# A GpSimd indirect step waits for the landing of the step two ahead of it

## Chip, cores and metric

One core of one Trainium2 chip runs the whole program. The metric is the device time in microseconds, median of the runs. TensorE is called PE in the rows, VectorE DVE, ScalarE ACT, GpSimd POOL and SyncE SP.

## The reference, cut to what matters

Two transformer layers run over x of 32 batches x 256 tokens x 128 features. Layer 0 is an RWKV mixer and an FFN. Layer 1 is a 16-head attention and a mixture of 8 experts, of which each token takes 2. Each of the four parts has its own modulation (shift, scale and gate by batch). The change lies in the experts' part, which the reference states densely:

```
for e in range(NUM_EXPERTS):
    expert_mask = jnp.any(top_idx == e, axis=-1)
    h = jax.nn.relu(flat_x @ W1[e] + b1[e])
    y = h @ W2[e] + b2[e]
    w = router_weights[:, e] * expert_mask.astype(x.dtype)
    final_output = final_output + y * w[:, None]
```

## The kernel before

The 8192 tokens are 16 chunks of 512 (NT = 4 tiles of 128). Every engine walks an order written out by hand (ORDER, a list of named steps for each engine), and waits only on semaphores. A step's number below is its place among the steps of its name. Steps of the letters A, E, B, C, G and R are layer 0, the attention and the router; they fill the span up to about 1435 us, and the experts' steps are mixed in from about 560 us on.

The experts' part works in four groups of 5, 5, 4 and 2 chunks, which have 47, 47, 39 and 23 tiles of 128 slots.

- S_slot (DVE, L1693) computes the slot of every token's two copies, once a group is routed.
- S_ld (SP, L603) loads the normed chunk into sx, two buffers. S_sc (POOL, L751) scatters it to x_slots in DRAM: two steps a chunk, one for each choice of expert, and each step is four indirect DMAs, one for each tile of 128 rows of 512 bytes.
- M_ldx (SP, L615) loads four slot tiles (a quad), after every scatter of its group has landed. M_w (SP, L628) loads one tile's expert weights. M_t (PE, L1048) turns a quad, M_u (PE, L1023) and M_d (PE, L1036 and L1040) are the tile's two products, and M_st (SP, L632) stores the quad to y_slots. Tiles 133 to 155 and quads 34 to 39 are the last group's.
- K_g (POOL, L770) gathers a chunk's rows from y_slots into kg: again two steps of four indirect DMAs a chunk, after every M_st of the chunk's group has landed. K_sum and K_out (DVE, L1717 to L1731) weigh, add and gate them, K_st (SP, L647) stores the output. K_ldx (SP, L642 and L643) loads the residual chunk and its gate.
- The gathers have four buffers (kg, the halves of bhs, and bqk), but chunks 0 to 9 all use the first. Chunks 10, 11 and 12 take the other three, 13 the first again, then 14 and 15 those of 10 and 11. The first step of a chunk waits until its buffer's last output is stored (k_st).

POOL has one walk over all 64 indirect steps: S_sc0-19, K_g0-9, S_sc20-27, K_g10-13, S_sc28, K_g14, S_sc29, K_g15, S_sc30, S_sc31, K_g16-31. The steps K_g28 to K_g31 belong to the last group and have no such wait; every other step, before its first DMA, waits in landed() for the step just ahead of it in this walk:

```
walk = [k for k in steps("Pool") if k[0] in ("S_sc", "K_g")]
return dict(zip(walk[1:], walk))
```

In SP's order the steps of this stage stand in one queue. From the middle of the tail: M_ldx33 M_w126 M_w127 K_st7 K_ldx8 M_w128 M_w129 M_ldx34 M_st30 M_w130-136 M_st31 K_st8 M_w137 M_ldx35 M_w138 M_st32 M_w139 K_ldx9 K_ldx10 M_ldx36 M_st33 M_w140-143 M_ldx37 K_ldx11 M_st34 M_w144 K_ldx12 K_ldx13 M_w145 M_st35 M_ldx38 M_w146-152 K_st9 M_ldx39 M_w153 K_ldx14 M_w154 K_st10 K_ldx15 K_st11 M_st36 M_w155 M_st37 K_st12 M_st38 M_st39 K_st13 K_st14 K_st15.

Of the kernel before, what the change touches and what calls it, by code (L numbers as in the profile page):

```python
# [13 lines left out]
ACT = mybir.ActivationFunctionType  # L14
# [7 lines left out]
NT = N // P  # L22
# [11 lines left out]
SIZES = (5, 5, 4, 2)  # L34
# [11 lines left out]
FIRST_CHUNK = [sum(SIZES[:g]) for g in range(GROUPS)]  # L46
# [37 lines left out]
e_dx e_xr e_xk e_xv e_r e_th e_k e_v e_ky e_m e_exp e_dv e_att e_wo e_x1 e_norm e_tp e_xn  # L84
e_fk e_rl e_sq e_fr e_th2 e_vk e_aq e_y e_ga e_out
b_ldm b_norm b_tp b_h b_w1 b_hs b_w2 b_x2 b_st b_q b_k b_t b_qk b_p b_r b_stq b_v b_va
c_ldq0 c_ldq1 c_rows0 c_rows1 c_s c_mx c_mp c_mt c_mT c_s2 c_p c_pv c_o c_ot c_ctx c_ct c_cT c_wo c_y c_ldm c_st
r_ldm r_z0 r_h0 r_hn r_tp r_h r_rt r_lg r_dm r_e r_info r_sth
s_zero s_tot s_pre s_base s_slot s_tile s_ldx0 s_ldx1 s_sc0 s_sc1
m_ldx0 m_ldx1 m_ldx2 m_ldx3 m_ldx4 m_ldx5 m_st0 m_st1 m_st2 m_st3 m_st4 m_st5 m_w0 m_w1 m_w2 m_w3 m_w4 m_w5 m_w6 m_w7 m_w8 m_w9 m_w10 m_w11 m_w12 m_w13 m_tp m_x m_h m_r m_y m_o  # L90
k_ld0 k_ld1 k_ld2 k_ld3 k_g0 k_g1 k_g2 k_g3 k_sum k_out k_st0 k_st1 k_st2 k_st3
vec
""".split()

# [49 lines left out]
def indirect_before():  # L144

    walk = [k for k in steps("Pool") if k[0] in ("S_sc", "K_g")]
    return dict(zip(walk[1:], walk))

class Count:  # L150
# [13 lines left out]
def program(nc, a):  # L164
    ctx = ExitStack()
    with ctx:
# [211 lines left out]
        def k_set(c):  # L378

            return k_sets[c], k_sets[:c + 1].count(k_sets[c])  # L380
# [33 lines left out]

        def scattered(g, k):

            return 16 * 2 * NT * len([c for c in range(FIRST_CHUNK[g] + SIZES[g]) if c % 2 == k])

        def rows(dram, i):
            return dram[i * N:(i + 1) * N, :].rearrange("(t p) d -> p t d", p=P)  # L420
# [4 lines left out]
        with nc.Block() as block:  # L425
# [63 lines left out]
            def _(sp):  # L489
                for s, i in steps("SP"):  # L490
# [108 lines left out]
                    if s == "S_ld":  # L599
                        sp.wait_ge(S["r_sth"], 16 * (i + 1))  # L600
                        if i >= 2:
                            sp.wait_ge(S[f"s_sc{i % 2}"], 16 * 2 * NT * (i // 2))
                        sp.dma_start(sx[:, i % 2, :, :], rows(x_h, i)).then_inc(S[f"s_ldx{i % 2}"], 16)  # L603

                    if s == "M_ldx":
                        g, t, j, n = first_of(i)
                        for k in range(2):
                            sp.wait_ge(S[f"s_sc{k}"], scattered(g, k))
                        k, use = x_slot(i)
                        if use > 1:  # L610
                            sp.wait_ge(S[f"m_st{k}"], 16 * (use - 1))
                        elif k >= MXS:

                            sp.wait_ge(S["e_vk"], 2 * CHUNKS)
                        sp.dma_start(quads[k][:, 0:n, :], x_slots[g][j * P:(j + n) * P, :]  # L615
                                     .rearrange("(t p) d -> p t d", p=P)).then_inc(S[f"m_ldx{k}"], 16)
# [36 lines left out]
            def _(pool):  # L653
# [10 lines left out]
                def landed(s, i):  # L664

                    if (s, i) not in before_:
                        return
                    s_, i_ = before_[s, i]
                    c_, k_ = divmod(i_, 2)
                    if s_ == "S_sc":  # L670
                        pool.wait_ge(S[f"s_sc{c_ % 2}"], 16 * NT * (2 * (c_ // 2) + k_ + 1))
                    if s_ == "K_g":
                        z_, n_ = k_set(c_)
                        pool.wait_ge(S[f"k_g{z_}"], 16 * NT * (2 * (n_ - 1) + k_ + 1))

                for s, i in steps("Pool"):
                    if s == "I_set":
# [64 lines left out]
                    if s == "S_sc":  # L742
                        c, k = divmod(i, 2)
                        if i == 0:
                            pool.wait_ge(S["s_zero"], 16 * GROUPS)
                        if k == 0:
                            pool.wait_ge(S["s_slot"], GROUP_OF[c] + 1)
                            pool.wait_ge(S[f"s_ldx{c % 2}"], 16 * (c // 2 + 1))
                        landed(s, i)
                        for t in range(NT):  # L750
                            pool.indirect_dma_start(  # L751
                                out=x_slots[GROUP_OF[c]],
                                out_offset=bass.IndirectOffsetOnAxis(ap=sslot[:, c, k, t:t + 1], axis=0),
                                in_=sx[:, c % 2, t, :], in_offset=None).then_inc(S[f"s_sc{c % 2}"], 16)
                    if s == "K_g":
                        c, k = divmod(i, 2)
                        z, n = k_set(c)
                        if k == 0:
                            for m in range(len(quads)):
                                if stored(GROUP_OF[c], m):  # L760
                                    pool.wait_ge(S[f"m_st{m}"], stored(GROUP_OF[c], m))
                            if n > 1:
                                pool.wait_ge(S[f"k_st{z}"], 16 * (n - 1))
                            elif z:

                                pool.wait_ge(S["r_h0"], CHUNKS)
                        if GROUP_OF[c] < GROUPS - 1:
                            landed(s, i)
                        for t in range(NT):
                            pool.indirect_dma_start(  # L770
                                out=kg[z][:, k, t, :], out_offset=None, in_=y_slots[GROUP_OF[c]],
                                in_offset=bass.IndirectOffsetOnAxis(ap=sslot[:, c, k, t:t + 1], axis=0)
                            ).then_inc(S[f"k_g{z}"], 16)

            @block.scalar
            def _(act):
# [7 lines left out]
                for s, i in steps("Activation"):  # L784
# [120 lines left out]
                    if s == "G_ct":  # L905
                        act.wait_ge(S["c_ct"], i + 1)
                        if i:
                            act.wait_ge(S["c_wo"], i)
                        act.activation(ccT[:, :], CO[:, :], ACT.Copy).then_inc(S["c_cT"], 1)

                    if s == "R_h":
                        act.wait_ge(S["r_tp"], i + 1)
# [34 lines left out]
            def _(pe):  # L947
# [109 lines left out]
                for s, i in steps("PE"):  # L1057
# [166 lines left out]
                                            cP[:, (4 * i + g) % 8, :], start=(sc_ == 0), stop=(sc_ == 1))  # L1224
                        ins.then_inc(S["c_pv"], 1)
                    if s == "G_o":
                        pe.wait_ge(S["c_o"], i + 1)
                        for j in range(4):
                            ins = pe.transpose(CO[:, j * P:(j + 1) * P], cos_[:, j * P:(j + 1) * P], ident[:, :])
                        ins.then_inc(S["c_ot"], 1)  # L1230
# [5 lines left out]
                                               ident[:, :])  # L1236
                        ins.then_inc(S["c_ct"], 1)
                    if s == "G_wo":
                        pe.wait_ge(S["c_cT"], i + 1)
                        bias_rows(CO, BO)  # L1240
                        for t in range(NT):
                            ins = pe.matmul(CO[:, t * P:(t + 1) * P], ccT[:, t * P:(t + 1) * P], woT[:, :],
# [38 lines left out]
            def _(dve):  # L1281
# [42 lines left out]
                for s, i in steps("DVE"):  # L1324
# [387 lines left out]
                    if s == "K_sum":  # L1712
                        k, n = k_set(i)
                        g_, w_ = kg[k], rinfo[:, i, :, :]
                        dve.wait_ge(S[f"k_g{k}"], 16 * 2 * NT * n)
                        for t in range(NT):
                            v(dve.tensor_scalar(g_[:, 0, t, :], g_[:, 0, t, :], w_[:, t, P1:P1 + 1], None, ALU.mult))  # L1717
                        v.wait()
                        for t in range(NT):
                            ins = dve.scalar_tensor_tensor(g_[:, 0, t, :], g_[:, 1, t, :], w_[:, t, P2:P2 + 1],  # L1720
                                                           g_[:, 0, t, :], ALU.mult, ALU.add)
                        ins.then_inc(S["k_sum"], 1)
                    if s == "K_out":
                        k, n = k_set(i)
                        g_ = kg[k]
                        dve.wait_ge(S["k_sum"], i + 1)
                        dve.wait_ge(S[f"k_ld{k}"], 32 * n)
                        v(dve.tensor_tensor(by_batch(g_[:, 1, :, :]), by_batch(g_[:, 0, :, :]),
                                            per_batch(km[k], g_), ALU.mult))
# [290 lines left out]
```

## Time and profile before

| | us |
|---|---|
| median of 3 runs | 1640.79 (1640.04 to 1642.62) |
| the profiled execution | 1635.33, its span 1633.4 |
| PE busy | 1352.7 (83%) |
| DVE busy | 1093.5 (67%) |
| ACT busy | 993.4 (61%) |
| POOL busy | 544.0 (33%) |

Times of rows are microseconds from the span's start. The shares of busy time are means over stages with different limits; the last 200 us are a stage of their own, without DVE's and ACT's layer work.

### The profile page before, as it was taken

Reading aid. Unit: us, or ns where it says so; the run is one execution under the profiler, and the core shown is the slowest. Engines: PE = TensorE matmul, PEld = TensorE weight load, DVE = VectorE, ACT = ScalarE, POOL = GpSimd, SP = SyncE. Lnnn points to the kernel's source line nnn. Section 1 sums busy time; section 2 is a strip of 40 time slices with the busy share of each in tenths; the row PEclk is TensorE's granted clock in tenths of the full one; section 3 lists DMA queues with packets and bytes.
Section 4 is the critical chain, followed back from the end, with each engine's and each line's share of the span. In section 5 each row is a group of like instructions: output and inputs, shape, how many; then the busy total and the mean of one; then the engine's idle time right before and its main releaser. Section 6 shows DMA issues by size and latency. Waiting matters only on the chain.

```text
span 1633.4 us, 26721 instructions
## 1 busy us (share of the span) xinstructions
PE 1352.7 (83%) x8354; PEld 857.3 (52%) x8354; DVE 1093.5 (67%) x2943; ACT 993.4 (61%) x2295; POOL 544.0 (33%) x589
## 2 busy tenths in 40 slices
PE   3366997888888778999999988999989998986680
PEld 1233443544444444767666543466656655776570
DVE  4568889898788988767677888778846644220113
ACT  1354766577575647787787675677666666653350
POOL 1133213222122465121212137725430144334345
PEclk7677888978899889999999998899999999998795
DMA  4012134215240333446455432345656566886872
GB/s 125 7 36 68 48 106 141 81 31 158 57 127 23 108 100 103 132 146 179 137 155 151 126 106 78 117 118 177 171 157 188 171 189 206 273 268 216 242 230 75
DMA packets 202036, 217.67 MB, mean 133 GB/s; under 512 B 17418, under 2 KB 167525, under 8 KB 199592
## 3 DMA queue, kind: packets, MB, share of 16 engines
q1 hardware_dynamic: 193704, 199.18, 40.7%
q0 software_dynamic: 8192, 16.79, 3.3%
q8 instruction: 68, 1.11, 0.3%
q14 instruction: 72, 0.59, 0.1%
HBM read 161.18 MB, written 53.94 MB: 132 GB/s over the span
## 4 chain that ended last, share of the span: by engine, by line
PE 37%; DVE 13%; issue 9%; POOL 8%; DMA 6%; ACT 5%; another core or an unknown queue 0%; SPq 0%; POOLq 0%; ACTq 0%; DVEq 0%
PE bank L1040 6%; PE bank L1223 5%; PE bank L1207 4%; PE bank L1023 4%; PE bank L1191 3%; DVE cmx L1576 3%; POOL kg L770 3%; DMA kg<-y_slots,sslot 3%; POOL x_slots L751 2%; DMA x_slots<-sx,sslot 2%; PE bank L1159 2%; POOL bhs L770 2%; PE bank L1119 1%; PE bank L1146 1%; PE bank L1167 1%
## 5 line engine op out<-in xcount | busy, mean ns | idle before, releaser
L1576 DVE TENSOR_REDUCE cmx<-bank 128x2 f32<-128x512 f32 x512 | 328.2, 682 | 89.5 <-PE bank L1191 82.8
L898 ACT ACTIVATE wide<-bank 128x512 f32<-128x512 f32 x512 | 281.2, 607 | 74.0 <-PE bank L1207 63.9
L1207 PE MATMUL bank<-wide 75*128 75x512 bf16 x512 | 179.5, 416 | 25.5 <-DVE cmx L1576 14.6
L1191 PE MATMUL bank<-wide 72*128 72x256 bf16 x1024 | 180.7, 284 | 23.8 <-DVE cmx L1576 20.4
L751 POOL DMA_INDIRECT x_slots<-sx,sslot x128 | 127.2, 994 | 111.8 <-issue 36.2
L1191 PEld LDWEIGHTS bank<-wide 72*128 72x128 bf16 x1024 | 91.5, 101 | 135.3 <-issue 62.5
L1223 PE MATMUL bank<-wide,bva 128*32 128x512 f32 x1024 | 144.2, 642 | 3.3 <-ACT wide L898 1.9
L937 ACT ACTIVATE mH<-bank,mW 128x128 f32<-128x128 f32 x376 | 107.8, 376 | 60.5 <-PE bank L1023 55.6
L1023 PE MATMUL bank<-mT,mW 128*128 128x128 f32 x872 | 120.2, 281 | 12.7 <-DMA mW<-in_wexp 6.7
L1023 PEld LDWEIGHTS bank<-mT,mW 128*128 128x128 f32 x872 | 108.7, 193 | 33.1 <-issue 11.9
L1207 PEld LDWEIGHTS bank<-wide 75*128 75x128 bf16 x512 | 49.5, 105 | 133.2 <-ACT wide L898 62.0
L770 POOL DMA_INDIRECT kg<-y_slots,sslot x88 | 85.7, 974 | 99.1 <-issue 34.0
L658 POOL TENSOR_TENSOR brs<-bvar,half 128x4 f32<-128x4 f32 x32 | 33.8, 1057 | 243.3 <-DVE bvar L1292 243.2
L1040 PE MATMUL bank<-mW,mH 128*128 128x128 f32 x752 | 108.9, 288 | 0.0
L1146 PE MATMUL bank<-bh,w 128*128 128x512 f32 x128 | 85.8, 758 | 13.8 <-ACT bhs L874 7.5
L1040 PEld LDWEIGHTS bank<-mW,mH 128*128 128x128 f32 x752 | 91.0, 191 | 6.3
L944 ACT ACTIVATE mX<-bank 128x128 f32<-128x128 f32 x120 | 33.6, 280 | 91.3 <-PE bank L1040 82.2
L730 POOL TENSOR_TENSOR bqk<-bqk,bp 128x768 f32<-128x768 f32 x32 | 53.5, 1672 | 103.7 <-ACT bp L884 103.6
L1119 PE MATMUL bank<-axk,fwk 128*128 128x512 f32 x128 | 70.7, 661 | 11.9 <-DVE axk L1295 10.2
L1717 DVE TENSOR_SCALAR kg<-kg,rinfo 128x128 f32<-128x128 f32 x44 | 9.7, 284 | 102.8 <-DMA kg<-y_slots,sslot 102.8
L874 ACT ACTIVATE bhs<-bank,col 128x512 f32<-128x512 f32 x64 | 44.3, 693 | 43.2 <-PE bank L1146 42.9
L1159 PE MATMUL bank<-w,bhs 128*128 128x128 f32 x512 | 65.6, 284 | 0.0
(296 smaller groups left out, 2801.1 us busy)
## 6 DMA issues: line engine op xcount, KB each, us to landing
mW<-in_wexp SPq DMA_DIRECT2D x109, 514.0 KB
wide<-q_parts SPq DMA_DIRECT2D x32, 576.0 KB
inner<-in_wexp SPq DMA_DIRECT2D x31, 514.0 KB
wide<-in_wexp SPq DMA_DIRECT2D x16, 514.0 KB, 5.5
mX<-x_slots SPq DMA_DIRECT2D x27, 256.0 KB
y_slots<-mX SPq DMA_DIRECT2D x27, 256.0 KB
q_parts<-bp SPq DMA_DIRECT2D x32, 192.0 KB
x_slots<-mH SPq DMA_DIRECT2D x2, 3072.0 KB, 11.0
```

The source lines that it names most:

```text
L751: pool.indirect_dma_start(out=x_slots[GROUP_OF[c]], out_offset=bass.IndirectOffsetOnAxis(ap=sslot[:, c, k, t:t + 1], axis=0), in_=sx[:, c ...
L770: pool.indirect_dma_start(out=kg[z][:, k, t, :], out_offset=None, in_=y_slots[GROUP_OF[c]], in_offset=bass.IndirectOffsetOnAxis(ap=sslot[: ...
L898: act.activation(cP[:, i % 8, :], bank[seat["G_s", i]][:, :], ACT.Exp, scale=SCALE).then_inc(S["c_p"], 1)
L937: act.activation(hidden[z][:, c * P:(c + 1) * P], bank[seat[k]][:, c * P:(c + 1) * P], ACT.Relu, bias=w_[:, FC * P + c:FC * P + c + 1]).th ...
L1023: ins = pe.matmul(ps[:, c * P:(c + 1) * P], weights[w_][:, c * P:(c + 1) * P], mT[:, q % 2, j * P:(j + 1) * P], start=True, stop=True)
L1040: ins = pe.matmul(ps[:, 0:P], hidden[z][:, c * P:(c + 1) * P], weights[w_slot(i)[0]][:, o:o + D], start=False, stop=(c == FC - 1))
L1146: pe.matmul(ps[:, :], w1[:, j * P:(j + 1) * P], bh[:, :], start=True, stop=True).then_inc(S["b_w1"], 1)
L1159: ins = pe.matmul(ps[:, t * P:(t + 1) * P], bhs[:, c, t * P:(t + 1) * P], w2[:, c, :], start=False, stop=(c == FC - 1 and t == NT - 1))
L1191: ins = pe.matmul(ps[:, j * T:(j + 1) * T], cQ[0:SROWS, z, h, tt * P:(tt + 1) * P], cK[0:SROWS, z, h // G, :], start=True, stop=True)
L1207: pe.matmul(ps[:, :], cK[0:KROWS, z, g, sc_ * P:(sc_ + 1) * P], cQ[0:KROWS, z, h0:h0 + 2, :], start=True, stop=True).then_inc(S["c_s2"], 1)
L1223: ins = pe.matmul(CO[32 * g:32 * g + 32, :], bva[:, c % 2, b * 2 + sc_, g, :], cP[:, (4 * i + g) % 8, :], start=(sc_ == 0), stop=(sc_ == 1))
L1576: dve.tensor_reduce(cmx[:, u % 2, tt, 2 * hp:2 * hp + 2], bank[seat["C_s", i]][:, :].rearrange("p (j t) -> p j t", j=2), AX_X, ALU.max, ne ...
```

## The change

Three edits go together. indirect_before() pairs each indirect step with the step two ahead in the walk, so two steps may be in flight. Because steps of one chunk may then land in either order, each half (k = 0 or 1) of a chunk parity has a semaphore of its own: s_sc00 to s_sc11 for the scatters, k_g00 to k_g11 for the gathers, which were counted by buffer. As a k_g semaphore is now shared by buffers, the first step of a chunk c from the third chunk on waits for K_out of chunk c - 2. To pay for the semaphores, k_sum and c_cT go: K_out waits on DVE's own counter, and the copy of G_ct counts on c_o.

```
-    return dict(zip(walk[1:], walk))
+    return dict(zip(walk[2:], walk))
...
-                            sp.wait_ge(S[f"s_sc{i % 2}"], 16 * 2 * NT * (i // 2))
+                            for k in range(2):
+                                sp.wait_ge(S[f"s_sc{i % 2}{k}"], 16 * NT * (i // 2))
...
-                            sp.wait_ge(S[f"s_sc{k}"], scattered(g, k))
+                            for j_ in range(2):
+                                sp.wait_ge(S[f"s_sc{k}{j_}"], scattered(g, k))
...
-                        pool.wait_ge(S[f"s_sc{c_ % 2}"], 16 * NT * (2 * (c_ // 2) + k_ + 1))
+                        pool.wait_ge(S[f"s_sc{c_ % 2}{k_}"], 16 * NT * (c_ // 2 + 1))
...
-                        z_, n_ = k_set(c_)
-                        pool.wait_ge(S[f"k_g{z_}"], 16 * NT * (2 * (n_ - 1) + k_ + 1))
+                        pool.wait_ge(S[f"k_g{c_ % 2}{k_}"], 16 * NT * (c_ // 2 + 1))
...
+                            if c >= 2:
+
+                                pool.wait_ge(S["k_out"], c - 1)
...
-                        act.activation(ccT[:, :], CO[:, :], ACT.Copy).then_inc(S["c_cT"], 1)
+                        act.activation(ccT[:, :], CO[:, :], ACT.Copy).then_inc(S["c_o"], 1)
...
-                        pe.wait_ge(S["c_o"], i + 1)
+
+                        pe.wait_ge(S["c_o"], i + i // 4 + 1)
...
-                        pe.wait_ge(S["c_cT"], i + 1)
+                        pe.wait_ge(S["c_o"], 5 * (i + 1))
...
-                        dve.wait_ge(S[f"k_g{k}"], 16 * 2 * NT * n)
+                        for j_ in range(2):
+                            dve.wait_ge(S[f"k_g{i % 2}{j_}"], 16 * NT * (i // 2 + 1))
...
-                        ins.then_inc(S["k_sum"], 1)
+                        v(ins)
...
-                        dve.wait_ge(S["k_sum"], i + 1)
+                        v.wait()
```

## Rows read from the trace of the kernel before

**Rows 1.** The page's chain that ended last, share of the span by engine.

```profile
PE 37%; DVE 13%; issue 9%; POOL 8%; DMA 6%; ACT 5%; another core or an unknown queue 0%; SPq 0%; POOLq 0%; ACTq 0%; DVEq 0%
```

**Rows 2.** Windows: stretch, its us, busy us by engine (instructions), clock, DMA share, GB/s.

```profile
1405.00:1477.00 72.00, 63.88 (x486) 56.26 (x486) 19.36 (x77) 41.17 (x144) 26.09 (x27) 1.00 0.87 270
...
1477.00:1592.00 115.00, 84.22 (x573) 72.95 (x571) 17.30 (x52) 46.95 (x169) 45.99 (x48) 0.88 0.72 228
1592.00:1633.00 41.00, 0.00 (x0) 0.00 (x0) 13.54 (x39) 0.00 (x0) 23.30 (x24) 0.51 0.26 75
```

**Rows 3.** Waits of POOL, 1405 to 1634: us in total, times, longest.

```profile
POOL kg L770 <- DMA kg<-y_slots,sslot: 15.6, 4, 5.8
POOL bhs L770 <- DMA bhs<-y_slots,sslot: 14.0, 3, 5.2
...
POOL kg L770 <- DMA x_slots<-sx,sslot: 9.3, 3, 4.1
...
POOL x_slots L751 <- DMA kg<-y_slots,sslot: 7.8, 2, 4.1
...
POOL x_slots L751 <- DMA x_slots<-sx,sslot: 3.9, 1, 3.9
```

**Rows 4.** Timeline of POOL: S_sc28, K_g14, K_g16, K_g18 and K_g28 begin.

```profile
1445.81 1.01 POOL L751 DMA_INDIRECT x_slots<-sx,sslot  x1 [11.69 <-DVE sslot L1693]
...
1454.70 0.97 POOL L770 DMA_INDIRECT kg<-y_slots,sslot  x1 [4.05 <-DMA x_slots<-sx,sslot]
...
1497.33 0.97 POOL L770 DMA_INDIRECT kg<-y_slots,sslot  x1 [2.06 <-DMA x_slots<-sx,sslot]
...
1520.34 0.94 POOL L770 DMA_INDIRECT kg<-y_slots,sslot  x1 [8.21 <-DMA out_dram<-kg]
...
1605.36 0.94 POOL L770 DMA_INDIRECT bhs<-y_slots,sslot  x1 [0.30 <-issue]
```

**Rows 5.** Chain: last DMA of K_g17, K_g19 and K_g31, start and us to landing.

```profile
1511.19 2.43 DMA kg<-y_slots,sslot
...
1534.51 6.30 DMA kg<-y_slots,sslot
...
1624.61 2.43 DMA bhs<-y_slots,sslot
```

**Rows 6.** Timeline of SP: M_w126/127, K_st7, M_ldx34, K_st8, M_ldx35, K_st9, K_st12.

```profile
1471.71 3.24 SPq L628 DMA_DIRECT2D inner<-in_wexp  x2
1482.69 0.40 SPq L647 DMA_DIRECT2D out_dram<-kg  x1
...
1496.60 0.38 SPq L615 DMA_DIRECT2D mX<-x_slots  x1
...
1517.17 0.40 SPq L647 DMA_DIRECT2D out_dram<-kg  x1
...
1518.80 0.36 SPq L615 DMA_DIRECT2D mX<-x_slots  x1
...
1562.03 0.43 SPq L647 DMA_DIRECT2D out_dram<-kg  x1
...
1595.21 0.38 SPq L647 DMA_DIRECT2D out_dram<-bqk  x1
```

**Rows 7.** Timeline of PE: M_u128, M_t35, M_u155 and the last matmuls.

```profile
1490.17 1.56 PE L1023 MATMUL bank<-mT,mW 128*128 128x128 f32 x8 [4.10 <-DMA mW<-in_wexp]
...
1522.92 1.09 PE L1048 MATMUL bank<-ident,mX 128*128 128x128 f32 x4 [10.38 <-DMA mX<-x_slots]
...
1587.81 1.13 PE L1023 MATMUL bank<-mT,mW 128*128 128x128 f32 x8 [2.61 <-DMA mW<-in_wexp]
...
1590.33 1.16 PE L1040 MATMUL bank<-mW,axr 128*128 128x128 f32 x8
```

**Rows 8.** First group's scatters: POOL's wait, 555 to 640; PE's timeline.

```profile
POOL x_slots L751 <- DMA x_slots<-sx,sslot: 12.8, 5, 5.3
```

```profile
613.37 3.70 PE L1119 MATMUL bank<-axk,fwk 128*128 128x512 f32 x4 [4.98 <-DVE axk L1295]
```

More of the change, by code:

```diff
@@ L86 @@
 b_ldm b_norm b_tp b_h b_w1 b_hs b_w2 b_x2 b_st b_q b_k b_t b_qk b_p b_r b_stq b_v b_va
-c_ldq0 c_ldq1 c_rows0 c_rows1 c_s c_mx c_mp c_mt c_mT c_s2 c_p c_pv c_o c_ot c_ctx c_ct c_cT c_wo c_y c_ldm c_st
+c_ldq0 c_ldq1 c_rows0 c_rows1 c_s c_mx c_mp c_mt c_mT c_s2 c_p c_pv c_o c_ot c_ctx c_ct c_wo c_y c_ldm c_st
 r_ldm r_z0 r_h0 r_hn r_tp r_h r_rt r_lg r_dm r_e r_info r_sth
-s_zero s_tot s_pre s_base s_slot s_tile s_ldx0 s_ldx1 s_sc0 s_sc1
+s_zero s_tot s_pre s_base s_slot s_tile s_ldx0 s_ldx1 s_sc00 s_sc01 s_sc10 s_sc11
 m_ldx0 m_ldx1 m_ldx2 m_ldx3 m_ldx4 m_ldx5 m_st0 m_st1 m_st2 m_st3 m_st4 m_st5 m_w0 m_w1 m_w2 m_w3 m_w4 m_w5 m_w6 m_w7 m_w8 m_w9 m_w10 m_w11 m_w12 m_w13 m_tp m_x m_h m_r m_y m_o
-k_ld0 k_ld1 k_ld2 k_ld3 k_g0 k_g1 k_g2 k_g3 k_sum k_out k_st0 k_st1 k_st2 k_st3
+k_ld0 k_ld1 k_ld2 k_ld3 k_g00 k_g01 k_g10 k_g11 k_out k_st0 k_st1 k_st2 k_st3
 vec
@@ L415, in scattered @@
         def scattered(g, k):
-            return 16 * 2 * NT * len([c for c in range(FIRST_CHUNK[g] + SIZES[g]) if c % 2 == k])
+            return 16 * NT * len([c for c in range(FIRST_CHUNK[g] + SIZES[g]) if c % 2 == k])
         def rows(dram, i):
@@ L753, in _ @@
                                 out_offset=bass.IndirectOffsetOnAxis(ap=sslot[:, c, k, t:t + 1], axis=0),
-                                in_=sx[:, c % 2, t, :], in_offset=None).then_inc(S[f"s_sc{c % 2}"], 16)
+                                in_=sx[:, c % 2, t, :], in_offset=None).then_inc(S[f"s_sc{c % 2}{k}"], 16)
                     if s == "K_g":
@@ L772, in _ @@
                                 in_offset=bass.IndirectOffsetOnAxis(ap=sslot[:, c, k, t:t + 1], axis=0)
-                            ).then_inc(S[f"k_g{z}"], 16)
+                            ).then_inc(S[f"k_g{c % 2}{k}"], 16)
             @block.scalar
```

## Prediction

> **What bounds the kernel now.** I read the chain that ended last first. PE carries 37% of it, POOL and the DMAs 14% together [rows 1], and asked by stretch these 14% lie in two places: the first group's scatters (555 to 610 us) and everything after 1420 us. The windows show the second: up to 1477 PE is busy 64 of 72 us, from 1477 to 1592 only 84 of 115 us, and in the last 41 us not at all, while the DMA engines, at 0.87 of their time before 1477, fall to 0.72 [rows 2]. So the tail waits for something that is neither PE nor bandwidth. POOL's own waits name it: landings of its indirect DMAs, 50.6 us in these five groups of 13 waits [rows 3]. The reader is to see in POOL's timeline that a step is 4.84 us of issuing (1445.81 to 1454.70 less the 4.05 of waiting), and that the next one starts only after a landing [rows 4]. The chain shows what a landing is, from the start of a step's last DMA: 2.43 us twice, 6.30 us in the busiest stretch [rows 5].
>
> PE is tied to this chain through SP's queue, in which loads for PE stand behind stores for POOL. K_st7 held SP from 1474.95 (the end of the weight issues ahead of it) to 1482.69; M_ldx34 waited for the last scatter until 1496.60; K_st8 held it until 1517.17, with M_ldx35 1.6 us behind [rows 6]. PE pays 4.10 us for the first, 10.38 us for the last, and 2.61 us at the end [rows 7].
>
> **The change part by part.** Four issues stay four issues; nothing is added to POOL but waits. Each step in place of "step ahead has landed" waits "step two ahead has landed", which leaves a whole step of issuing (5.0 to 5.1 us with the 0.3 us gap) for the landing. The step after the next can begin 1.25 + 5.0 = 6.25 us after the start of a step's last DMA, so a landing of 2.43 us is hidden entirely and one of 6.30 us costs next to nothing, if two steps in flight land as one does. Bounds for the landing: 2.43 below, 6.30 above [rows 5].
>
> The first gain is at the scatters. S_sc28 starts at 1445.8 as before, since DVE's slots release it [rows 4]. Six steps (S_sc28, K_g14, S_sc29, K_g15, S_sc30, S_sc31) at 5.1 us are issued by 1476.4, and the last scatter has landed by 1478 to 1482, where it was 1496.6 [rows 6]. M_ldx34 goes out some 15 us earlier, before PE, which would come to it at about 1491, needs it.
>
> The second is at K_st7. Chunk 7's gathers are issued by 1466.2 (four steps) and land 2.4 to 6.3 us after the last one's start. From K_g17's landing (1511.19 + 2.43) to K_st8 (1517.17) lie 3.55 us of DVE and SP [rows 5, 6], so K_out7 is done by 1472 to 1475 and SP issues K_st7 at once, at 1475. From K_st8 to K_g18 took 3.2 us [rows 4, 6], so K_g16 starts at 1478.2 instead of 1497.3. M_w128 leaves 7.7 us earlier, and PE's 4.10 us go.
>
> The third, and the one that counts, is at K_st8. K_g16 and K_g17 run without a wait between them: the last DMA starts 9.0 us later, at 1487.2, lands at 1489.7 to 1493.5, and K_st8 goes at 1493.2 to 1497.1, which is 20 to 24 us earlier. M_ldx35 follows 1.6 us later and M_t35 4.1 us after that [rows 6, 7], 1499 to 1503. PE itself, without its 4.10 us, comes to M_t35 at 1486.1 plus five tiles at 2.7 us (62 us for 23 tiles, worked out in the next paragraph), 1499.6. So the 10.38 us become 0 to 3, and the last group's tiles start at 1500 to 1504, not at 1523.8.
>
> Its 23 tiles took from 1523.8 to 1591.5, 67.7 us. Off this go the 2.61 us of M_w155, which K_ldx15 and K_st11 held back, and part of the slow clock that followed the 10.38 us of idling: the granted clock was 0.88 in this stretch against 1.00 before [rows 2, 7]. I take 3 us for it, with 0 as its low end. That is 62 us, or 65 without the clock's part, so that PE ends between 1562 and 1569. The DMA engines speak against the low end. They worked 0.72 x 115 = 83 us between 1477 and 1592; the same bytes at the 0.87 of the stretch before take 95 us, until 1572 [rows 2]. I take 1570.
>
> From there: the last quad's store goes about 1 us after PE's end (K_st12, which held it until 1595.2, is ready long before), and K_g28 starts 3.2 us after it, at 1574 where it was 1605.4. From K_g28's start to the span's end are 16 issues, a landing, DVE and a store: 1633.4 - 1605.4 = 28.0 us [rows 4], with no landed wait in them, so unchanged. The end is 1602, 31 us earlier.
>
> POOL's own chain must be ready by then. K_g18 starts at 1497 to 1500, eight steps at 5.0 us take it to 1540, K_g26 then waits for K_st9, which SP reached 38.2 us after M_u133 [rows 6], now 1541, plus 3.2; K_g27 is issued by 1554. That is 20 us of slack: POOL would have to need 7.5 us a step before it sets the end.
>
> Upstream the waits are shorter and mostly covered. In the first group POOL waits 12.8 us for landings, and PE then stands 4.98 us for the chain that goes through the POOL step behind them [rows 8]. S_sc6 also needs S_ld3, which SP issues at about the old time, so I take 2.5 us of the 4.98. The three other groups' waits lie beside a busy PE; I count 0 to 2 us, below 0 nothing, as no wait is longer there. With half a microsecond: 2 to 3 us.
>
> The rest costs nothing that I can price. S_ld and M_ldx wait on two semaphores for one, in the 1.2 us that SP needs anyway between K_st8 and M_ldx35 [rows 6]; below 0.1 us each. K_out(c - 2) is implied by the buffer's store up to chunk 10, and in chunks 11 to 15 it is 3.5 us behind a gather whose landing is 5 us past: what is queued behind it (K_g) finds it met. K_out's wait is on its own engine. The renamed c_o counts wait for what stands earlier in PE's order.
>
> Of a DMA's length the Trainium skill ("DMA: Bandwidth & Descriptors", section "Anatomy of one DMA") says about 2.0 us fixed, most of it the receipt of the last write, plus bytes over 436e3. For 64 KB that is an estimate of 2.15 us. The unloaded rows of 2.43 agree and the loaded one of 6.30 doesn't [rows 5]; by the page alone K_st8 would go at 1493, inside the bounds above.
>
> The sum: 31 + 2.5 = 33 us off. It is made against the profiled execution's 1635.33 (span 1633.4, 1.9 us around it), which lies 5.5 us below the median of the runs; 1640.8 - 33 = 1608. The likeliest case's own range is 1598 (PE 1562, upstream 4) to 1617 (all high ends, SP losing a few us more).
>
> **The rivals.** A, the software queue is served at a rate and not after a latency: K_g19's four DMAs took 3.75 us of issues and 6.30 more, 10 us, and if under load that is 2.5 us of service each, a second step in flight only queues behind the first. What remains of each removed wait is the gap from a landing to the next issue, about 1 us with its first DMA's latency. The 13 waits give 13 us [rows 3], 1628. For it speaks that the long landings lie where DMA is busiest; against it that K_g28 to K_g31 issue 16 DMAs at 1.25 us and the last lands in 2.43 all the same [rows 5], though at a DMA share of 0.26 [rows 2]. 
>
> B, the weight loads become the bound: the tail's last 28 tiles are short of bandwidth, at the 228 GB/s that the stretch had on average [rows 2], and PE ends at 1580 to 1588. K_g28 at 1588 gives 17 us and upstream 2: 1621.
>
> C, slower: the denser scatters and gathers take so much from the weight loads after 1445 that PE ends later than it did. The price is known: PE would have to lose more than the 31 us over 28 tiles, 1.1 us on each 2.9, that is a rate down from 228 to 165 GB/s, where the stretches before show 270. From there on it decides, not earlier.
>
> D, no change: something else holds SP at K_st7 and K_st8 (the residual loads, or landings over 10 us when two steps share the queue), and the pair of steps lasts what it lasted. 1640.
>
> **How the numbers follow.** The main case 0.68, A 0.13, B 0.13, C 0.03, D 0.03. Faster by over 0.2% (3.3 us, about what these runs tell from no change) are the first three, 0.94; within it 0.03; slower 0.03. The range goes from the main case's low end to A's time with its bounds: 1597 to 1629.
>
> **What would show it.** After 1445 POOL's steps follow each other by 5.0 to 5.5 us, with waits for landings under 12 us in total where they were 50.6. K_st8 stands at about 1495, M_t35 has no wait above 4 us, the DMA share between 1477 and PE's end is over 0.85, and K_g28 is released by the store of the last quad and not by POOL. If landings go to 10 us it is A; if PE waits for mW, inner or wide over the last group it is B. I am wrong if K_st8 is later than 1505.

## The result, and the profile after

The changed kernel took 1695.20 us (median of 4 runs, 1691.56 to 1696.52), the kernel before 1640.76 beside it: a ratio of 1.0338 with a 95% interval of 1.0319 to 1.0358. That is 54 us slower, where 33 faster were forecast. The profiled execution took 1694.17 us (span 1692.4).

The page's chain by engine comes first; [rows 1] had nothing for an unknown queue and 14% for POOL and DMA.

```profile
PE 46%; DVE 12%; ACT 8%; another core or an unknown queue 6%; issue 6%; POOL 1%; DMA 1%; SPq 0%; POOLq 0%; ACTq 0%; DVEq 0%
```

POOL and the DMAs are nearly off the chain, but 6% (some 100 us) is put down to nothing that the profile knows. The waits of the changed kernel (us in total, times, longest) name who it is. "Remote" stands where the profile finds no instruction and no DMA that ended just before the wait did; below such waits are called ended by nothing:

```profile
ACT mX L948 <- remote: 54.1, 7, 16.7
...
ACT bhs L878 <- remote: 13.5, 2, 9.2
...
DVE rlg L1631 <- remote: 10.6, 1, 10.6
```

ACT has 112.8 us of such waits and DVE 15.1; SP's queue has 36.1 more, all for PE's line 1044. The timelines of ACT and of PE, around 1500 us, show one (the columns are those of [rows 4]):

```profile
1493.41 0.28 ACT L948 ACTIVATE mX<-bank 128x128 f32<-128x128 f32 x1 [3.65 <-remote]
1493.58 1.14 ACT L941 ACTIVATE axr<-bank,mW 128x128 f32<-128x128 f32 x4
1506.82 0.28 ACT L948 ACTIVATE mX<-bank 128x128 f32<-128x128 f32 x1 [12.10 <-remote]
1506.99 1.14 ACT L941 ACTIVATE axk<-bank,mW 128x128 f32<-128x128 f32 x4
1514.53 0.60 ACT L930 ACTIVATE mT<-bank 128x512 f32<-128x512 f32 x1 [6.40 <-remote]
```

```profile
1494.93 1.80 PE L1044 MATMUL bank<-mW,axr 128*128 128x128 f32 x8
1496.53 1.06 PE L1052 MATMUL bank<-ident,ah 128*128 128x128 f32 x4
1507.15 2.08 PE L1027 MATMUL bank<-mT,inner 128*128 128x128 f32 x8 [9.56 <-ACT mX L948]
```

ACT's copy into mX waits in the program for one thing, the matmuls of line 1044. They end at 1496.73; the copy starts at 1506.82, and PE's next tile, which waits for that copy, 0.3 us behind it. All that time POOL issues indirect DMAs (24 from 1479.90 to 1511.7, the last 20 every 1.25 to 1.5 us without a gap over 0.3 us). The same picture stands at 1588.75 to 1605.44 (16.69 us), beside 24 issued from 1571.25 to 1602.5, and at 578.71 (9.21 us), beside 12. I call this the hold.

**Whose event is late.** The trace also holds the semaphore updates themselves, and they say more than "remote" does. In the recorded run ACT and DVE have 23 such waits of over 1 us, and each is for a semaphore that PE counts up. The update that ends the wait is recorded, within 0.03 us of the start of the waiting instruction; it is late against the matmuls that send it. The one for the copy above is recorded at 1506.80, 10.1 us after their end at 1496.73. Fifty of PE's updates come over 1.5 us after the last matmul that could have sent them, the latest 16.9 us after. ACT's 1,843 and POOL's 322 all come within 0.01 us of their instruction's end. Ends of matmuls are modelled, but the order alone shows it: PE's transposes (line 1052, from 1496.53) were followed by seventeen more matmuls from 1507.15 to 1511.45, and only at 1514.50 is the transposes' update recorded, with two more of PE within 0.2 us and 2.8 us after POOL's last issue. So what is held is PE's semaphore updates. ACT, DVE and SP stand still because they wait for PE.

Of POOL's waits for landings in [rows 3] none is left, and the last landing of the chain is as long as in [rows 5]:

```profile
1682.31 2.44 DMA bhs<-y_slots,sslot
```

PE's waits of 4.10 and 10.38 us [rows 7] have given way to 9.56, 4.92 and 12.67 us for ACT. The rows that answer to [rows 4] and [rows 6], timelines of POOL and of SP:

```profile
1479.90 1.01 POOL L752 DMA_INDIRECT x_slots<-sx,sslot  x1 [12.86 <-DVE sslot L1698]
...
1535.51 0.97 POOL L774 DMA_INDIRECT kg<-y_slots,sslot  x1 [23.85 <-DMA out_dram<-kg]
...
1559.81 0.94 POOL L774 DMA_INDIRECT kg<-y_slots,sslot  x1 [14.58 <-DMA out_dram<-kg]
...
1663.32 0.94 POOL L774 DMA_INDIRECT bhs<-y_slots,sslot  x1 [18.51 <-DMA y_slots<-mX]
```

```profile
1529.95 0.43 SPq L649 DMA_DIRECT2D out_dram<-kg  x1
...
1535.03 0.38 SPq L617 DMA_DIRECT2D mX<-x_slots  x1
...
1552.12 1.14 SPq L649 DMA_DIRECT2D out_dram<-kg  x1
...
1554.59 0.36 SPq L617 DMA_DIRECT2D mX<-x_slots  x1
```

S_sc28 starts 34.1 us later than in [rows 4], K_g28 58.0 later. So 34 us are lost before the tail, most of them (25.8) between 1325 and S_sc28, where 16 indirect DMAs run without a break, and 24 in the tail. The windows, as in [rows 2]:

```profile
1405.00:1477.00 72.00, 63.02 (x460) 50.74 (x459) 19.31 (x82) 41.77 (x130) 18.13 (x19) 0.95 0.76 238
1477.00:1592.00 115.00, 74.01 (x460) 64.37 (x460) 17.23 (x55) 37.46 (x134) 53.82 (x56) 0.77 0.67 214
1592.00:1664.00 72.00, 49.85 (x332) 43.82 (x330) 10.26 (x30) 28.07 (x100) 16.32 (x18) 0.81 0.53 172
```

PE and the DMAs both fell: PE 74.0 us of 115 where it had 84.2, DMA share 0.67 for 0.72. Neither is the bound: PE waits for ACT, the weight loads wait in SP's queue, and PE's granted clock falls from 0.88 to 0.77 with its idling.

### The profile page after: what moved, and what is told of

The parts are those of the page before. It is cut to its first block, busy times and chain, and to the rows that moved or that the text cites. A ratio compares the mean times of both kernels' runs of the same rounds, so it can differ in the third digit from the quotient of the medians.

```text
span 1692.4 us, 26787 instructions
## 1 busy us (share of the span) xinstructions
PE 1375.4 (81%) x8354; PEld 875.1 (52%) x8354; DVE 1094.2 (65%) x2943; ACT 993.4 (59%) x2295; POOL 544.9 (32%) x589
## 4 chain that ended last, share of the span: by engine, by line
PE 46%; DVE 12%; ACT 8%; another core or an unknown queue 6%; issue 6%; POOL 1%; DMA 1%; SPq 0%; POOLq 0%; ACTq 0%; DVEq 0%
PE bank L1044 9%; PE bank L1027 7%; PE bank L1227 5%; PE bank L1211 5%; DVE cmx L1581 4%; PE bank L1195 3%; PE bank L1163 2%; PE bank L1150 2%; PE bank L1123 2%; ACT wide L902 1%; PE bank L1139 1%; PE bank L1040 1%; PE bank L1012 1%; PE bank L1171 1%
## 5 line engine op out<-in xcount | busy, mean ns | idle before, releaser
L1603 DVE RECIPROCAL crs<-bank 128x16 f32<-128x16 f32 x64 | 16.2, 253 | 80.8 <-PE bank L1234 72.5
```

## The experiments

Theory H, in terms of the waits: the other engines are held while POOL issues more than about 8 indirect DMAs without a pause. Rivals: K, the new counts and waits cost it; B, the denser scatters and gathers take bandwidth from the weight loads; and, after the first results, C, it belongs to the chip.

Eighteen runs were made, on six chips, the kernel before beside each. The chips fall into two kinds by three marks that agree in every run: the time of the kernel before (1630 to 1631, or 1641 to 1650), and the last two columns. "Held" is the sum of ACT's and DVE's remote waits in us; "records" is the number of semaphore updates by DMAs that the trace holds.

```
run (chip)               us       before   ratio [95%]              held   records
e5  changed kernel (15)  1584.80  1630.80  0.9728 [0.9703, 0.9753]    0    16,008
e6  7 unlanded     (15)  1586.02  1630.80  0.9732 [0.9714, 0.9749]    0    15,998
e2  6 unlanded     (15)  1592.04  1631.29  0.9755 [0.9739, 0.9772]    0    16,019
e7  5 unlanded     (15)  1605.42  1630.80  0.9853 [0.9836, 0.9871]    0    16,033
e1  one ahead      (15)  1631.47  1631.29  1.0008 [0.9992, 1.0025]    0    16,034
e8  tail one ahead (15)  1624.02  1630.80  0.9962 [0.9949, 0.9976]    0    16,020
e3  1.1 us pause   (15)  1603.08  1631.29  0.9822 [0.9806, 0.9839]    0    16,006
e16 0.2 us break   (12)  1589.08  1630.25  0.9754 [0.9724, 0.9784]    0    16,004
recorded result    (?)   1695.20  1640.76  1.0338 [1.0319, 1.0358]  127.9  11,942
e9  changed kernel  (3)  1711.65  1645.51  1.0400 [1.0351, 1.0450]  138.6  11,877
e10 three ahead     (3)  1708.31  1645.51  1.0395 [1.0349, 1.0442]  128.1  11,889
e12 6 unlanded     (10)  1682.00  1649.94  1.0192 [1.0124, 1.0260]   99.2  11,937
e18 0.2 us break   (13)  1716.55  1646.86  1.0437 [1.0393, 1.0480]  120.9  11,861
e14 1.1 us pause    (5)  1626.50  1641.00  0.9904 [0.9878, 0.9930]   25.2  12,230
e13 3.3 us pause    (5)  1687.12  1641.00  1.0273 [1.0218, 1.0328]    9.7  12,813
bursts: e4 (15) 1626.85, before 1631.29; e17 (12) 1627.63, before 1630.25;
        e11 (10) 1690.39, before 1649.94; e15 (5) 1647.48, before 1641.00
        held 0, 0, 77.1 and 20.4; records 16,586, 16,776, 12,753 and 12,900
```

The updates give a fourth mark. In every run on chips 12 and 15 PE's latest update comes 0.06 us after its matmul. On the others 8 (e13) to 51 (e10) come over 1.5 us late. The kernel before, on the chip on record, has 12, none over 2.2 us. Each burst kernel was timed once. Chip 15 was met twice and every other numbered chip once, so that "the chip" may also be the occasion.

**Is it the bookkeeping?** e1 keeps all of the change but the distance:

```diff
-    return dict(zip(walk[2:], walk))
+    return dict(zip(walk[1:], walk))
```

> The changed kernel with everything kept (counts of their own for the halves, the wait for K_out, the merged counters) except that a step waits for the step one ahead again. Theory H (the hold): while POOL issues more than about 8 indirect DMAs without a pause, ACT, DVE and SP stand still; the loss is in the runs of back-to-back steps alone, so this kernel is at the kernel before, 1640 +- 5 us, and ACT's waits that no engine of the trace ends fall from 95 us and more to about 10. Rival K (the counts): the new waits or merged counters cost it; then this kernel stays near 1695.

1.0008: the separate counts, the wait for K_out and the merged counters cost nothing, as forecast.

**Fewer unlanded, or a pause.** e2 makes a step wait for the step one ahead before its third DMA; e6 does it before the fourth, e7 before the second. e3 puts POOL's own small power ahead of each step that waits.

```diff
                         for t in range(NT):
+                            if t == 2:
+                                landed(s, i, one_ahead)
                             pool.indirect_dma_start(
```

```diff
+                            pool.tensor_tensor(idle_[:, :], onesf[:, 0:NT], half[:, :], ALU.pow)
```

> The changed kernel, in which a step also waits for the step one ahead before its own third DMA, so that at most 6 indirect DMAs are unlanded instead of 8. Theory H in its form 'what counts is how many are unlanded': the waits for nothing in the trace fall to about 10 us, and the time to 1625 to 1645. Theory H in its form 'what counts is that POOL issues without a pause': where a landing takes 2.4 us the third DMA waits for almost nothing, the pauses are 0 to 3 us, and part of the hold stays: 1640 to 1680. Rival B (bandwidth: the denser scatters and gathers take it from the weight loads): it follows the mean rate of issue, which hardly falls, 1680 to 1695.

> The changed kernel with one tiny VectorE-like operation of POOL itself (a power of 128x4, 1.04 us by the rows of such operations) ahead of every step that waits for the one two ahead. It waits for no landing, and two steps are still in flight. Form 'without a pause': a pause of 1.1 us after each 4 DMAs lets the others go on, 1620 to 1650, and ACT's waits for nothing in the trace fall under 20 us. Form 'how many unlanded': 1680 to 1700, since the DMAs in flight are the same. Rival B: 1680 to 1695.

Both were much faster than the kernel before, and no wait in any trace of this chip is remote. Either both mended the hold, or there was none on this chip.

**The hold by itself.** e4 adds gathers that nobody reads to the kernel before.

```diff
+                    for j in range(12):
+                        if apart_ and j and j % 4 == 0:
+                            pool.wait_ge(S["k_g0"], 16 * (12 * n + j))
+                        pool.indirect_dma_start(out=..., in_=x_slots[0], ...)
```

> The kernel before (one step ahead), with 36 gathers added that nobody reads, in three stretches of 26 to 34 us in which POOL was idle while PE, ACT and DVE worked: 12 back to back of 64 KB each, 12 back to back of 4 KB each, and 12 of 64 KB in three lots of 4, each lot after the landing of the lot ahead. Theory H: ACT or DVE stands still for 5 to 10 us, with no engine that ends the wait, in the first and the second burst from about 8 DMAs in, and not in the third; the time rises by 5 to 20 us. Rival B: the 4 KB burst costs nothing, and the third costs about what the first does. If none of the three shows a wait, the hold needs something else that the tail has.

None of the three held anybody, and the time did not rise. This fell against theory H, so the changed kernel had to be timed again beside its neighbours.

> The changed kernel itself, once more, beside its neighbours. With 8 DMAs unlanded and a tiny operation of POOL between steps the time was 1603; with at most 6 unlanded and nothing between, 1592; and 12 gathers back to back in the middle of the kernel held nobody. Theory H (the hold by an unbroken run of indirect DMAs) in what is left of it: it needs a run of over 12, as only this kernel's tail has, and this run gives 1685 to 1700 again, with the waits for nothing. Rival C (the chip or the occasion: the loss belongs to the chip that timed it and not to the kernel): here it gives 1590 to 1610, like its two neighbours.

> The changed kernel with the wait for the step one ahead before a step's fourth DMA, so that at most 7 are unlanded. Between 6 (1592) and 8. Theory H: by then 3.8 us of issuing cover most landings, runs are nearly unbroken, and the time lies between 1592 and 1695, at 1600 to 1660. Rival C: 1588 to 1600, the same as with 6.

> The same with the wait before a step's second DMA: at most 5 unlanded. 1.25 us of a landing of 2.4 to 6.3 us are covered, a third of what 7 cover: both theories give a third to a half of the 39 us that 6 gained, 1605 to 1622.

1584.8: the same program is 2.7% faster here. Its POOL issues 20 indirect DMAs without a break from 1437 us on, and ACT keeps its pace beside them. With 5, 6, 7 and 8 unlanded the time falls from 1605 to 1592, 1586 and 1585; 7 take nearly all that two ahead give. e8 is one ahead again from S_sc28 on:

```diff
+    at = walk.index(("S_sc", 28))
+    return dict(list(zip(walk[2:at], walk)) + list(zip(walk[at:], walk[at - 1:])))
```

> The changed kernel, two ahead up to the scatter of chunk 13, and from the scatters of the last group (S_sc28) on one ahead. Theory H: the long runs are all after 1445 us except one of 12 in the first group, so nearly all of the 54 us goes, 1625 to 1650, and the first group's share alone is left. Rival C: what the tail gained is given back, the first group's 2 to 8 us stay, 1622 to 1632.

1624: so about 7 of the 46 us come from before the tail, and 39 from the tail.

**Another chip.** e9 is the changed kernel once more, e10 waits three ahead.

> The changed kernel a third time. It took 1695 us where it was first timed (kernel before 1641 beside it) and 1585 where the experiments ran (1631 beside it). Theory C (the occasion: one chip's event path loses and delays what indirect DMAs send, the kernel is the faster one elsewhere): 1580 to 1592 if this is the chip of the experiments, and either this or about 1695 on another. Theory H (the kernel's unbroken runs hold the other engines by themselves): 1685 to 1700; after the last run I give it little.

> The changed kernel with each step waiting for the one three ahead: up to 12 indirect DMAs unlanded. If the hold has a threshold of unlanded or unbroken DMAs that lies higher on this chip, it shows here as waits for nothing and a time over 1600. If landings are all that a step waits for, two ahead has hidden them already (0.3 and 0.8 us of such waits are left in its tail), and this one takes the same 1585 within 3 us.

On chip 3 the loss is back, larger than on record, with the same waits:

```profile
ACT mX L948 <- remote: 57.1, 7, 18.5
...
DVE rlg L1631 <- remote: 10.6, 1, 10.6
```

Three ahead is no different from two. So the chip, or the occasion, decides whether there is a hold, and the kernel whether it is met.

**The burst on such a chip.** e11 adds a fourth burst, of 8.

> The burst kernel again (the kernel before, with gathers added that nobody reads, in stretches where POOL was idle beside a working PE, ACT and DVE), now with four: 8 back to back of 64 KB, 12 back to back of 64 KB, 12 back to back of 4 KB, and 12 of 64 KB in lots of 4, each after the landing of the lot ahead. On the chip of the first eight runs 12 back to back held nobody. If this is a chip of the other kind (kernel before at 1640 or more, the changed one 4% slower): theory P (there an unbroken run of indirect DMAs holds the other engines, whatever the bytes) says that ACT or DVE stands still for 3 to 15 us, ended by nothing recorded, beside the two bursts of 12 and not beside the lots of 4, with 8 near the edge. Rival Q (bytes: what these chips lack is DMA bandwidth) says that the 4 KB burst costs nothing. Rival R (only the tail's weight loads together with the gathers do it) says that no burst costs anything.

The starts of the four bursts in POOL's timeline (lines that follow at 1.25 us are left out), then what ACT and DVE waited for in these stretches:

```profile
652.16 1.03 POOL L690 DMA_INDIRECT kg<-x_slots,sslot  x1 [0.53 <-issue]
...
734.86 1.04 POOL L690 DMA_INDIRECT kg<-x_slots,sslot  x1 [0.52 <-issue]
...
833.37 1.04 POOL L690 DMA_INDIRECT kg<-x_slots,sslot  x1 [0.52 <-issue]
...
932.66 1.04 POOL L690 DMA_INDIRECT kg<-x_slots,sslot  x1 [0.52 <-issue]
```

```profile
663.68 0.28 ACT L969 ACTIVATE mX<-bank 128x128 f32<-128x128 f32 x1 [3.35 <-remote]
...
752.10 1.14 ACT L962 ACTIVATE mH<-bank,mW 128x128 f32<-128x128 f32 x4 [5.65 <-remote]
...
849.11 0.28 ACT L969 ACTIVATE mX<-bank 128x128 f32<-128x128 f32 x1 [6.24 <-remote]
```

```profile
744.29 0.69 DVE L1601 TENSOR_REDUCE cmx<-bank 128x2 f32<-128x512 f32 x1 [5.07 <-remote]
...
752.14 0.69 DVE L1601 TENSOR_REDUCE cmx<-bank 128x2 f32<-128x512 f32 x1 [5.03 <-remote]
...
850.55 0.69 DVE L1601 TENSOR_REDUCE cmx<-bank 128x2 f32<-128x512 f32 x1 [15.97 <-remote]
```

On chip 15, in e4, the last of these DVE instructions stood beside the same 4 KB burst like this:

```profile
818.50 0.69 DVE L1600 TENSOR_REDUCE cmx<-bank 128x2 f32<-128x512 f32 x1 [6.27 <-PE bank L1215]
```

Twelve gathers of 4 KB hold DVE for 15.97 - 6.27 = 9.7 us more. The longest remote waits beside the twelve of 64 KB are 5.65 us (ACT) and 5.07 (DVE): rival Q, the bytes, falls. The unbroken 8 hold ACT for 3.35 us. Beside the three lots of 4, each after a landing, DVE has one wait of 3.84 us ended by nothing and ACT none. The whole kernel took 1690 us, 40 more than the kernel before beside it; on chip 15 the three bursts of e4 had cost nothing.

> The changed kernel with the wait for the step one ahead before each step's third DMA, at most 6 unlanded: 1592 on the chip where the changed kernel took 1585. On a chip of the other kind: if the number of unlanded DMAs makes the hold, with 6 instead of 8 most of it goes, 1590 to 1640; if it is POOL's unbroken issuing, the waits of 0 to 3 us in the middle of a step break the run in part, 1620 to 1690; if any rate above that of the kernel before is too much, 1690 to 1710. On the chip of the first runs: 1589 to 1595 again.

1682: two ahead with 6 unlanded is 1.9% slower than the kernel before on chip 10 (1.2 to 2.6%). It pauses only where a landing takes longer than two issues, and its trace has runs of 10 and 12.

**Which pause mends it.** e13 is e3 with three powers in place of one, e14 is e3 again. e15 breaks the bursts in the same way.

> The changed kernel with three tiny operations of POOL's own (1.04 us each, some 3.3 us in all) ahead of each step that waits for the one two ahead: no unbroken run is longer than 4 DMAs. On a chip of the second kind (kernel before at 1640 or more): if a pause in time is what lets the others through, it is at 1600 to 1645 and its trace has under 25 us of waits ended by nothing recorded; if the DMAs have to land first (a landing there takes 2.4 to 6 us), part of the hold stays, 1645 to 1690. On the first chip: a step every 8.3 us, where one ahead took 5.0 and a landing: 1605 to 1625.

> The same with one such operation, 1.1 us: 1603 on the first chip. On a chip of the second kind the step repeats every 6.1 us where the changed kernel's does every 5.0. If the hold grows with the backlog that a rate of over one DMA per some 1.6 to 2 us leaves, a fifth less rate takes a part of it away only: 1650 to 1700. If any break is enough: 1600 to 1645.

> The burst kernel with four bursts of 12 gathers of 64 KB, broken by POOL's own tiny operations (1.1 us each): one after each 4, one after each, three after each 4, two after each 4. On a chip of the second kind, where 12 unbroken ones held ACT and DVE for 5 us twice in one burst and 16 us in another: if a break itself is enough, none of the four holds anybody. If it is the mean rate, the first holds them nearly as long as an unbroken one (15 us of issuing become 17), the fourth for 0 to 5 us, and the second and third (2.4 and 2.1 us per DMA) not at all. On the first chip none holds anybody.

On chip 5 e14 is 1.0% faster than the kernel before, and its waits ended by nothing are 25 us where the unbroken kernels of other chips have 128 to 139. The unbroken kernel itself did not run on chip 5. That the chip is of the second kind is read from its marks, 20 late updates of PE in e14 among them; how long it would hold the unbroken kernel is not shown. In e15 one pause after each 4 leaves ACT and DVE alone beside the burst at 651 us, and beside the third burst (three pauses after each 4) cmx shows its 6.27 us, ended by PE, as on chip 15; beside the fourth, with two pauses, DVE has one such wait, 3.75 us. The expectation of a hold "nearly as long" for the first was wrong. A step of e14 in POOL's timeline:

```profile
1475.03 1.04 POOL L685 TENSOR_TENSOR idle_<-onesf,half 128x4 f32<-128x4 f32 x1
1476.26 1.02 POOL L787 DMA_INDIRECT kg<-y_slots,sslot  x1 [0.19 <-issue]
...
1482.31 1.05 POOL L764 DMA_INDIRECT x_slots<-sx,sslot  x1 [0.19 <-POOL idle_ L685]
```

e13, at 1687, is in the range of "the DMAs have to land first", but not for that reason. Its holds are gone (9.7 us); its steps repeat every 8.3 us whether or not anything has landed, and POOL's own operations stand behind them: ACT's waits for bqk grow from 19.9 us in e14 to 33.3, S_sc28 starts at 1502.6 for 1457.9, and from there to K_g28 it needs 155.7 us for 136.3. Where the rest of the 61 us between the two comes from stays open.

**Rate or break.** e16 and e18 are e14 with a multiplication of 0.2 us in place of the power; e17 breaks the bursts with it.

```diff
-                            pool.tensor_tensor(idle_[:, :], onesf[:, 0:NT], half[:, :], ALU.pow)
+                            pool.tensor_tensor(idle_[:, :], onesf[:, 0:NT], half[:, :], ALU.mult)
```

> The changed kernel with a break of one 0.2 us multiplication of 128x4 on POOL ahead of each step, where 1.1 us gave 1603 on the first chip and 1626 on one of the second kind. By the rows of the bursts a break of 0.2 us leaves the rate at 1.25 us per DMA. If any other instruction between the DMAs is enough to let the others through: no waits ended by nothing recorded, and 1588 to 1598 on the first chip, 1600 to 1620 on one of the second kind. If the rate makes the hold: the first chip as said, and 1670 to 1710 on one of the second kind.

> The burst kernel with four bursts of 12 gathers of 64 KB: broken by a 0.2 us multiplication after each 4, and after each one; by one 1.04 us power after the sixth; and after the eighth. On a chip of the second kind: if the rate makes the hold, the first holds ACT or DVE for 4 to 10 us; if an instruction between is enough, it doesn't, nor does the second; the last holds for 3 to 6 us, as the unbroken 8 did (3.4 us), and the third for 0 to 3. On the first chip none holds anybody.

> The changed kernel with the 0.2 us break once more, which took 1589 (kernel before 1630 beside it) where no hold occurs at all. On a chip of the second kind: 1600 to 1620 and no waits ended by nothing recorded if any instruction between the DMAs lets the others through; 1670 to 1710 if it is the rate of 1.25 us per DMA that holds them. On one of the first kind: 1586 to 1592 again, and the question stays open.

e16 and e17 met a chip of the first kind and could not answer. e18 met one of the second. Its timelines of POOL and ACT:

```profile
1504.14 0.95 POOL L787 DMA_INDIRECT kg<-y_slots,sslot  x1 [0.30 <-issue]
1505.11 0.21 POOL L685 TENSOR_TENSOR idle_<-onesf,half 128x4 f32<-128x4 f32 x1
1505.48 1.01 POOL L764 DMA_INDIRECT x_slots<-sx,sslot  x1 [0.16 <-issue]
```

```profile
1508.92 0.28 ACT L961 ACTIVATE mX<-bank 128x128 f32<-128x128 f32 x1 [4.12 <-remote]
1509.09 1.14 ACT L954 ACTIVATE axr<-bank,mW 128x128 f32<-128x128 f32 x4
1525.97 0.28 ACT L961 ACTIVATE mX<-bank 128x128 f32<-128x128 f32 x1 [15.75 <-remote]
```

On chip 13 a step every 5.1 to 5.5 us (about 1.3 us per DMA) with an instruction between is 4.4% slower than the kernel before, as the unbroken one is on chip 3; on chip 5 a step every 6.2 us (1.55 per DMA) is held nearly not at all. So it isn't enough that something stands between the DMAs. That time must pass is the likely reading, but it compares two chips.

## Why the prediction was wrong

**The step that failed** is the first of the change part by part: "nothing is added to POOL but waits". Of every step that was made denser I priced what it does to POOL's chain and to the landings, and priced at nothing what it does to ACT, DVE and SP. On the chip on record PE's semaphore updates came up to 16.9 us late beside the denser steps, and those who wait for PE paid 112.8 us (ACT), 15.1 us (DVE) and 36.1 us (SP's queue), in part at the same time. The sum's 33 us off became 54 on.

**The evidence that I leaned on was taken where it could not show this.** Against rival A I held that K_g28 to K_g31 issue 16 DMAs at 1.25 us without harm. They do so after 1605 us, where ACT and PE are busy for 0.00 us [rows 2]. In [rows 4] every other step of POOL stands behind a landing, so no unbroken run over 4 stood beside working engines. And the trace of before had a mark that I passed over, since it is small. The same kind of wait in the kernel before:

```profile
ACT mH L937 <- remote: 4.4, 2, 2.7
...
DVE cmx L1576 <- remote: 2.9, 2, 1.9
```

With the smaller ones it is 11.8 us. On chips of the first kind no run has any.

**The other steps, where there is no hold.** There the change gave 46 us. The forecast was 33, with a range of 12 to 44, so that even here the gain was underestimated, about half of it upstream and half in the tail. e5 on chip 15 tests the steps one by one, against e1 on the same chip (one ahead, S_sc28 at 1441.10). In e5, timelines of POOL, SP and PE:

```profile
1431.14 1.01 POOL L752 DMA_INDIRECT x_slots<-sx,sslot  x1 [11.47 <-DVE sslot L1698]
...
1464.16 0.97 POOL L774 DMA_INDIRECT kg<-y_slots,sslot  x1 [1.59 <-DMA out_dram<-kg]
```

```profile
1459.21 0.40 SPq L649 DMA_DIRECT2D out_dram<-kg  x1
...
1482.73 0.40 SPq L649 DMA_DIRECT2D out_dram<-kg  x1
...
1484.44 0.36 SPq L617 DMA_DIRECT2D mX<-x_slots  x1
```

```profile
1488.86 1.09 PE L1052 MATMUL bank<-ident,mX 128*128 128x128 f32 x4 [6.56 <-DMA mX<-x_slots]
```

- The landings: POOL's waits for them after 1405 us are 1.8 us in all, forecast under 12. Right, and right in the recorded run too, which has none.
- From S_sc28, K_st7 was forecast 29.2 us on and came after 28.1, K_st8 47 to 51 and came after 51.6. M_t35 waits 6.56 us where 0 to 3 were said (above 4 was to speak against me): PE came to it 51.2 us after S_sc28 and not 53.8, the tile 57.7 us after it, half a microsecond past the forecast's late end.
- PE's end, 62 to 65 us after M_t35: 62.7 (1551.6). The DMA share between 1477 and PE's end is 0.91, forecast over 0.85.
- K_g28 128 us after S_sc28: 123.2. One ahead needs 160.7 there, so the tail gave 37.5 us where 31 were forecast. The end, 28.0 us after K_g28, came after 29.1.
- Upstream: 10 us by S_sc28 between the two traces (7 by the medians of e8) for 2.5. Of the 10, 2.4 stand before the first scatter, and 3.6 and 3.5 in the second and third stretch between scatters, which I had counted at 0 to 2 together.
- Rival A, 13 us: 46 came. Rival B: PE, at 1580 to 1588, would have ended 77 us or more after M_t35. Rival C had the right sign and another mechanism; its price, over 31 us of PE time through bandwidth, was not what was paid, since 4 KB gathers hold no less than 64 KB ones. The other costs at nothing: e1, right.

The Trainium skill ("DMA: Bandwidth & Descriptors", section "Anatomy of one DMA") gives the estimate of 2.15 us for such a landing; the last ones of the recorded run and of e5 took 2.44 and 2.49 us, 0.3 above it: near, where the DMA engines are busy for 0.21 of the time (e5, from 1555 us). It would not have changed the outcome: landings were never what the change cost.

**What stays open.** Shown is that on some chips (3, 10, 13 and the one on record) PE's semaphore updates come late beside indirect DMAs issued at 1.25 to 1.3 us each, from some eight in a run on, whatever the bytes, and that ACT, DVE and SP wait for them; and that chips 12 and 15 don't have it. That 1.55 us per DMA nearly ends it was seen on chip 5 alone. Why POOL's issuing delays PE's updates, and not those of ACT, DVE or POOL, is not shown. (DVE's are prompt but for two, which stand in e5 as well.) One trait goes with it: traces of the held kind lack a fifth to a fourth of the semaphore updates by DMAs, and more than half of the indirect ones in the unbroken kernels (1,574 of 4,096 are there in the recorded run, 4,063 in e5). The lateness is no fault of the recording, since the waiting engines start only then. But the recording may be its cause: records go missing and updates come late in the same traces, and every run here has the span and clock that the recording gives. No run tells whether the hold occurs without it. Fetching of instructions is an unlikely path: in the recorded trace no instruction packet starts between 1481.4 and 1518.4 us, while ACT starts again at 1506.82. Why the chips differ is open too. So is whether a lower rate or a long enough break ends the hold: both changed together in e14.

## What to carry to other kernels

A wait that costs time on its own engine may be what paces that engine for all the others: before it is removed, look in the trace for a stretch where the denser pattern already runs beside busy engines, and count none that runs alone. When a result contradicts its own trace's arithmetic, time the same kernel on another chip before building on it. Read small waits that end by nothing as a warning, and look up when the awaited semaphore's update is recorded against the end of the instruction that sends it: that says whose event is late, where the waits only say who suffers. Here two ahead with a pause of 1.1 us per step is the version that was faster on both kinds of chip (0.982 on chip 15, 0.990 on chip 5); two ahead as it stands is 0.973 or 1.04, by the chip.

## What the runs showed of the hardware

- On the chip on record PE's semaphore updates come up to 16.9 us late (50 of them over 1.5 us) beside unbroken indirect DMAs of POOL; ACT's and POOL's come within 0.01 us. On chip 15 (e5) PE's latest comes after 0.06 us.
- The same program on two chips: 1584.8 and 1711.7 us, where the kernel before differs by 1% (1630.8 and 1645.5).
- Twelve back-to-back indirect gathers of 4 KB: DVE's wait beside them 15.97 us on chip 10 and 6.27 on chip 15.
- POOL itself never slows: in the recorded run its indirect DMAs follow at 1.25 us through both holds, and land: the last one of K_g15 starts at 1500.25, and DVE starts on what it brought at 1502.84, while ACT waits for PE's update.
